# Feed-forward batches set to 18 turns against the recurrence's 32 phases, and the relaying of p and k moved from ScalarE to GpSimd

## The reference, cut to what matters

```python
def step(S, inp):                       # the recurrence, 512 tokens in order
    q_t, k_t, v_t = inp
    S = S * lam
    err = v_t - jnp.einsum('bhk,bhkv->bhv', k_t, S)
    S = S + beta * (k_t[..., :, None] * err[..., None, :])
    o_t = jnp.einsum('bhk,bhkv->bhv', q_t, S)
    return (S, o_t)
...
h = jax.nn.silu(_tlin(x, w1_w, w1_s)) * _tlin(x, w2_w, w2_s)      # the feed-forward
h = jax.nn.gelu(_tlin(h, h1_w, h1_s), approximate=False)
h = jax.nn.gelu(_tlin(h, h2_w, h2_s), approximate=False)
return _tlin(h, w3_w, w3_s)
...
x = x + _L0_attn_ref(xn, ...) + _L0_ffn_ref(xn, ...)
```

## Time and profile before

| | us |
|---|---|
| median of three runs | 954.16 |
| the profiled execution, whole | 952.11 |
| its span | 950.4 |
| DVE busy in the span | 780.1 |
| PE busy | 787.3 |
| POOL busy | 597.3 |
| ACT busy | 588.6 |

### The profile page before, as it was taken

One profiled execution on the slowest core, in us unless ns is written; L12 is line 12 of the kernel. 1 busy time (PEld: TensorE's weight loads), 2 busy tenths in 40 slices (PEclk: granted clock), 3 DMA queues, 4 the chain that ended last, 5 costly groups with the idle time before them and its releaser, 6 DMA issues. The chain is left out here.

```text
span 950.4 us, 12821 instructions
## 1 busy us (share of the span) xinstructions
PE 787.3 (83%) x2956; PEld 499.2 (53%) x2956; DVE 780.1 (82%) x1573; ACT 588.6 (62%) x1079; POOL 597.3 (63%) x542
## 2 busy tenths in 40 slices
PE   5388888266989898998988799874899999999996
PEld 3234343145655666665565666542455655555654
DVE  5588887199999999999999999912788888888885
ACT  3487877368878797877879787632444434443431
POOL 0078888264665555566655566412887878878873
PEclk9999999668999999999999999895999999999999
DMA  5145554900505023050504101023112312213201
GB/s 143 55 167 204 206 203 181 197 14 1 123 11 99 22 51 81 11 121 11 110 11 87 46 16 39 11 61 123 38 57 64 102 55 73 93 55 99 67 12 33
DMA packets 121652, 74.98 MB, mean 79 GB/s; under 512 B 73490, under 2 KB 99996, under 8 KB 121628
## 3 DMA queue, kind: packets, MB, share of 16 engines
q1 hardware_dynamic: 119420, 72.98, 27.3%
q10 hardware_dynamic: 2208, 1.74, 0.6%
HBM read 41.14 MB, written 33.55 MB: 79 GB/s over the span
## 5 line engine op out<-in xcount | busy, mean ns | idle before, releaser
L958 POOL TENSOR_TENSOR f_hl<-f_h,f_hh 128x512 fp32r<-128x512 f32 x64 | 81.9, 1296 | 113.3 <-ACT f_hh L1057 113.2
L1354 POOL TENSOR_TENSOR l_kv<-l_qkv 128x1024 f32<-128x1024 f32 x64 | 125.0, 1952 | 21.3 <-PE l_ps_s L1564 21.3
L966 POOL TENSOR_TENSOR f_g<-f_a,f_b 128x512 f32<-128x512 f32 x64 | 81.5, 1284 | 65.5 <-ACT f_b L1046 65.5
L1132 PE MATMUL f_ps<-f_gh,w_hi 128*128 128x512 f32 x256 | 105.0, 410 | 10.3 <-POOL f_gl L958 5.2
L1132 PE MATMUL f_ps<-f_xh,w_hi 128*128 128x512 f32 x128 | 58.2, 455 | 65.2 <-ACT f_a L1042 51.5
L1132 PE MATMUL f_ps<-f_hh,w_hi 128*128 128x512 f32 x256 | 107.8, 421 | 0.0
L933 DVE TENSOR_TENSOR r_pg<-r_rec,r_pt 128x512 f32<-128x512 f32 x128 | 88.5, 692 | 20.1 <-ACT r_kb L1002 14.4
L939 DVE TENSOR_REDUCE r_rec<-r_pg 128x64 f32<-128x576 f32 x128 | 97.4, 761 | 7.2
L1407 ACT ACTIVATE l_qkv<-l_ps_q 128x512 f32<-128x512 f32 x64 | 38.3, 598 | 103.3 <-PE l_ps_q L1551 103.3
L1485 DVE TENSOR_TENSOR l_qs<-l_ps_s,l_qd 128x1024 f32<-128x1024 f32 x64 | 78.2, 1221 | 24.1 <-PE l_ps_s L1564 22.8
L942 DVE TENSOR_TENSOR r_kw<-r_rec,r_kb 128x512 f32<-128x512 f32 x128 | 88.5, 691 | 4.5
(11 more groups left out here) (183 smaller groups left out, 1986.6 us busy)
## 6 DMA issues: line engine op xcount, KB each, us to landing
p_x<-in_L_attn_x_dram SPq DMA_DIRECT2D x16, 256.0 KB, 2.9
scratch_xnT<-p_xnT SPq DMA_DIRECT2D x16, 256.0 KB, 3.0
scratch_K<-p_kout SPq DMA_DIRECT2D x16, 256.0 KB, 2.9
scratch_fac<-p_fac SPq DMA_DIRECT2D x16, 256.0 KB, 2.0
scratch_R<-p_rr SPq DMA_DIRECT2D x16, 256.0 KB, 2.0
scratch_P<-p_pp SPq DMA_DIRECT2D x16, 256.0 KB, 2.1
f_x<-scratch_xnT SPq DMA_DIRECT2D x16, 256.0 KB, 2.9
r_p<-scratch_P SPq DMA_DIRECT2D x16, 256.0 KB, 4.7
```

The source lines that it names most:

```text
L958: pool.tensor_tensor(lower, full, upper.bitcast(F32), ALU.subtract).then_inc(done, 1)
L966: pool.tensor_tensor(g_f[:, j, :], a_f[:, j, :], b_f[:, j, :], ALU.mult).then_inc(gate_ok, 1)
L1132: nc.tensor.matmul(bank, c.w_hi[:, weights[k], :], upper[k], start=k == 0, stop=False)
L1354: pool.tensor_tensor(dst, k, v, ALU.mult).then_inc(kv_ok, 1)
```

## The change

Turns and phases are now tied by points. A turn has two points (its start, and before L1061 of before), 36 in all for 18 turns (16 batches and two turns of tail), and `serve` at point p serves phase p*32/36 - 1 (rounded down) if that is a new one. Four points after the first serve nothing. So turn 0 has no phase to serve, turn 5 and turn 14 have none at their start (points 10 and 28), and the last phases are served in the tail. `lay_r` now lays r two phases ahead of the saved one, as before.

The relaying of p and k is moved to POOL (`lay_p`, `lay_k`, tensor_copy), after the four `f_hl` of batches 1, 3, 5, 7, 10, 12 and 14 for segments 1 to 7. For segment 0 POOL lays p ahead of its first `f_xl`, and ACT lays k. DVE waits for two semaphores in place of one. The loops of ACT, POOL and SP over the batches are written out; those of PE and DVE are as before. SP's stores and loads are sorted to the new points.

```diff
@@ scalar
-                    save_w(s, 1)
-                    if not last:
-                        lay_r(s, 1)
+                    serve(n, 1)
...
+                def serve(n, half):
+
+                    ended = (2 * n + half) * NPH // POINTS - 1
+                    before = (2 * n + half - 1) * NPH // POINTS - 1
+                    if ended > before >= -1:
+                        save_w(ended)
+                        if ended + 2 < NPH:
+                            lay_r(ended + 2)
...
-                lay_pk(0)
-                lay(0, 0)
-                batch(Slot(0), first=True)
-                batch(Slot(1), second=True)
-                with act.Fori(0, 3) as it:
...
+                lay_r(0)
+                lay_first_k()
+                lay_r(1)
+                for n in range(SLOTS):
+                    batch(n)
+                serve(SLOTS, 0)
                 result(Slot(SLOTS - 2))
+                serve(SLOTS, 1)
                 for o in range(NB):
                     last_hidden(Slot(SLOTS - 1), o)
+                serve(SLOTS + 1, 0)
                 result(Slot(SLOTS - 1))
+                serve(SLOTS + 1, 1)
+                save_w(NPH - 1)
@@ gpsimd
+                def lay_p(seg):
+
+                    u = seg % 2
+                    pool.wait_ge(seg_in[u], 48 * G * (seg // 2 + 1))
+                    for g in range(G):
+                        ins = pool.tensor_copy(tok_p[u][:, g, :, :].rearrange("p (b i) k -> p b i k", i=BLK),
+                                               seg_p[u][:, g, :, :].rearrange("p k (i b) -> p b i k", i=BLK))
+                    ins.then_inc(p_laid, 1)
...
+                lay_p(0)
                 input_rest(Slot(0))
...
+                for n in range(SLOTS):
+                    batch(Slot(n), more=n < SLOTS - 1)
+                    for seg in range(1, NSEG):
+                        if ((seg - 1) * SEGPH + 2) * POINTS // NPH // 2 == n:
+                            lay_p(seg)
+                            lay_k(seg)
@@ vector
-                        dve.wait_ge(pk_laid, it * 2 + (u + 1))
+                        dve.wait_ge(p_laid, it * 2 + (u + 1))
+                        dve.wait_ge(k_laid, it * 2 + (u + 1))
```

More of the change, by code:

```diff
@@ L787, in recur_and_feed_forward @@
     RING = 6
+    POINTS = 2 * (SLOTS + 2)
     with ctx:
@@ L831, in recur_and_feed_forward @@
         w_out = [sem(f"r_w_out{u}") for u in range(2)]
-        pk_laid, r_laid, w_saved = sem("r_pk_laid"), sem("r_laid"), sem("r_w_saved")
+        p_laid, k_laid, r_laid, w_saved = sem("r_p_laid"), sem("r_k_laid"), sem("r_laid"), sem("r_w_saved")
         m1_ok, w_ok, m2_ok, gain_ok, s_ok = sem("r_m1_ok"), sem("r_w_ok"), sem("r_m2_ok"), sem("r_gain_ok"), sem("r_s_ok")
@@ L877, in _ @@
                 load(1, 1)
[L878 to L890, removed]
-                            if not last:
[L892 to L903, removed]
+                for n in range(SLOTS + 2):
+                    if n < SLOTS - 1:
+                        next_x(Slot(n))
+                    ends = [seg for seg in range(NSEG) if (seg + 1) * SEGPH * POINTS // NPH in (2 * n, 2 * n + 1)]
+                    late = [seg for seg in ends if (seg + 1) * SEGPH * POINTS // NPH == 2 * n + 1]
+                    if n >= 2 and late:
+                        store_y(Slot(n - 2))
+                    for seg in ends:
+                        if seg < NSEG - 2:
+                            load_after(seg, seg % 2)
+                        store(seg, seg % 2)
+                    if n >= 2 and not late:
+                        store_y(Slot(n - 2))
+                store(NSEG - 1, (NSEG - 1) % 2)
                 sp.wait_ge(y_out, 16 * SLOTS + 16)
@@ L974, in hidden_rest, with lay_k @@
                     rest(h_f[:, o, :], h_h[:, o, :], h_l[:, o, :], hl_ok)
+                def lay_p(seg):
[5 more added lines that the diff above has]
+                    ins.then_inc(p_laid, 1)
+                def lay_k(seg):
+                    u = seg % 2
+                    for g in range(G):
+                        ins = pool.tensor_copy(blk_k[u][:, g, :, :, :], seg_k[u][:, g, :, :].rearrange("p k (i b) -> p b k i", i=BLK))
+                    ins.then_inc(k_laid, 1)
                 def batch(s, more=True):
@@ L988, in batch, with lay_r @@
                         hidden_rest(s, o)
+                lay_p(0)
                 input_rest(Slot(0))
-                with pool.Fori(0, SLOTS - 1) as it:
-                    batch(Slot(0, it))
-                batch(Slot(SLOTS - 1), more=False)
+                for n in range(SLOTS):
[4 more added lines that the diff above has]
+                            lay_k(seg)
             @block.scalar
             def _(act):
[L997 to L1008, removed]
+                def lay_r(phase):
+                    seg, at, q = phase // SEGPH, phase % SEGPH, phase % 2
+                    u = seg % 2
+                    if at == 0:
+                        act.wait_ge(seg_in[u], 48 * G * (seg // 2 + 1))
+                    if phase >= 2:
+                        act.wait_ge(w_ok, PH * (phase - 1))
                     act.activation(pg[q][:, :, :, :, DH].rearrange("p a vg i -> p vg a i"),
@@ L1011, in lay, with save_w, lay_first_k @@
                                    ACT.Copy).then_inc(r_laid, 1)
-                def lay_r(s, half):
-                    ahead = 2 * s.off + 1 + half
-                    u, at = (ahead // SEGPH) % 2, ahead % SEGPH
+                def save_w(phase):
+                    seg, at, q = phase // SEGPH, phase % SEGPH, phase % 2
+                    u = seg % 2
                     if at == 0:
[L1018 to L1030, removed]
+                        act.wait_ge(w_out[u], 16 * G * (seg // 2 + 1))
+                    act.wait_ge(s_ok, PH * (phase + 1) + 1)
                     act.activation(seg_w[u][:, :, :, at * TPH:at * TPH + TPH].rearrange("p v g t -> p (v g) t"),
                                    w_of[q], ACT.Copy).then_inc(w_saved, 1)
+                def lay_first_k():
+                    for g in range(G):
+                        ins = act.activation(blk_k[0][:, g, :, :, :], seg_k[0][:, g, :, :].rearrange("p k (i b) -> p b k i", i=BLK), ACT.Copy)
+                    ins.then_inc(k_laid, 1)
+                def serve(n, half):
[5 more added lines that the diff above has]
+                            lay_r(ended + 2)
                 def input_upper(s):
@@ L1066, in result, with batch @@
                     act.activation(y_t[:, :], y_at[:, :], ACT.Identity, scale=c.s3[:, :], bias=c.ob[:, :]).then_inc(y_ok, 1)
[L1068 to L1071, removed]
+                def batch(n):
+                    s = Slot(n)
+                    first, second, last = n == 0, n == 1, n == SLOTS - 1
+                    serve(n, 0)
                     silu(s, 0)
```

9 lines of the change are left out of this document (removed).

## The result

The changed kernel takes 941.6 us (median of 6 runs, 938.5 to 942.7) against 954.2 for the kernel before beside it (6 runs, 952.6 to 957.5): ratio 0.987, 95% interval 0.985 to 0.989, 12.6 us faster. The forecast was 950.0.

A forecast was written before the change was run, and what follows sets the result against it. DVE's recurrence was taken as the bound, with the feed-forward tail to win: 12.8 us less 1.1 lateness and 7.5 low clock is 4.2, so 947.9 profiled, stated as 950 against the 954.16 median; range 941 to 965.

The forecast's parts named there:

- The bound: DVE's recurrence bounds the stage while it runs: 434.6 us, 13.56 per phase; 17.0 us of feed-forward tail follow it.
- The end: After the recurrence, save and W stores take 5.4 us until the next stage's first load.
- The start: With POOL laying p beside ACT's r and k, DVE starts the recurrence at about 186.3, 1.3 us earlier.
- The turn without copies: An ACT turn without relaying needs 24.0 us, read from turn 12, with nothing left over at the new pace.
- The price of an output at low clock: PE's output takes 5.39 us instead of 3.69 when the granted clock falls, costing 1.7 us.
- the slower rival, copies too slow: POOL's copies become the bound: gain gone at 1.48 us a copy, 29 us slower at 2.7; chance 0.20.
- the turn with relaying on POOL: Four copies of 1.3 us make the gates 2.6 to 2.8 us late and six turns 25.4 us.
- the 1.1 us of lateness: At point 29, in turn 14's second half, service comes at 539.2 where DVE wants it at 538.1.
- the 7.5 us of low clock: PE's pauses ahead of z1 of j=3 lower the clock over outputs: 5.7 us plus 1.8 us.
- The formula for the turn: ACT's chain in a turn with copies: 27.08 - 4.07 (relaying) - 0.22 (wait for DVE) + 2.6 (gates late) = 25.4 us.
- the recurrence alone: Rival: clock holds or copies are near 1.07 us, 11.7 to 12.8 us won, time 942; chance 0.20.
- the alternation of turns: Sign: ACT's turns alternate between 24.0 and 25.4 us, or 25.7 where the output runs at low clock.

The follow-up runs named there:

- experiment 1: The changed kernel with the old pacing of 32 points instead of 36, relaying of p and k still on POOL: 953.86 us, ratio 0.998 to the kernel before.
- experiment 2: The changed kernel with 36 points, but p and k of segments 1 to 7 relaid by ACT again: 966.38 us, ratio 1.011 to the kernel before.
- experiment 4: The changed kernel with three unused copies more in each relaying on POOL, seven in all, 7.0 us: 958.15 us, ratio 1.003 to the kernel before.
- experiment 3: The changed kernel with a fifth, unused copy in each relaying on POOL, 5.1 us: 944.73 us, ratio 0.989 to the kernel before.
- experiment 5: The changed kernel with one unused ACT instruction of 0.57 us at the start of each turn: 946.65 us, ratio 0.993 to the kernel before.

## Why the prediction was wrong

**What held.** The bound: the recurrence is never faster than its 13.6 us per phase, and the gain can be no more than the tail less the last store (12.8 by the sum, 12.4 at equal landing). The end: 5.0 us, 5.4 forecast. The start: 1.3 us. The turn without copies: 24.0 us, read from one turn. The pace at which the points come due: 435.3/18 = 24.2 us, so these turns just fit. The price of an output at low clock: 1.7 us. Both parts of the change are needed (experiments 1 and 2), and the slower rival, copies too slow, is real with its waits at the very places (experiment 4), only from a price on that POOL doesn't have.

**The step that failed** is the turn with relaying on POOL: "I take 1.3, in the middle of the near ones", and with it 25.4 us for six turns, where 24.0 were measured; the 1.1 us of lateness and the 7.5 us of low clock were worked out from it, and both came to nothing. A copy takes 1.07 to 1.09 us by its groups and 1.01 from one to the next, which is the prediction's own lower bound, worked out from what is fixed in the two-input rows. That bound was the better supported one: the upper one supposed that nothing of a copy's 402 ns is fixed, against what those rows showed, and a fixed part hidden behind the operation before, the reason given for 1.3, speaks for less and not for more. That 1.07 was met to 0.01 us is luck in part, since the fixed part was borrowed from another operation. By the Trainium skill (GPSIMD Engine Reference, section 7: some 2.9 cycles per element for reads with a step over 8 bytes) a copy was estimated at 1.34 us. The runs don't agree for this form: 30 copies of 512 rearranged elements stand at 1.07 to 1.09, and the measurement decides.

**What hung on it.** The gates come 1.9 us late instead of 2.6 to 2.8. The formula for the turn then has another 0.75 us too much, as experiments 3 and 4 show, and the traces show most of it. It added the delay in full, but the second save comes 1.5 us late and not 1.9: ACT's own waits for the gates take up 0.36. And turn 11 of before did wait for DVE at its end, which the prediction denied. These rows of before stand ahead of the save at 513.44:

```profile
512.54 0.77 ACT L1057 ACTIVATE f_hh<-f_ps,t 128x512 fp32r<-128x512 f32 x1
513.04 0.36 DVE L952 SCALAR_TENSOR_TENSOR r_rec<-r_rec,lam,r_gain 128x128 f32<-128x128 f32 x1
```

The save starts 0.90 us behind the last `f_hh`, where 0.57 is usual, and right behind the end of DVE's block at 513.40; that is 0.33. So the turn with copies is 24.0, as the others. From that two terms fall. The lateness at point 29, 1.1 us: six turns shorter by 1.4 would have left ample room, but the wait for DVE at turn 9 and the low output behind it take most of it back; the serving there is at 538.72 where DVE wants it at 539.4, 0.7 us ahead. And the clock, 7.5 us, the largest term: it was priced with PE's pause of 1.9 us behind turns made longer by the copies. No such turn was left; the pauses are 1.42 us and the clock stays in all eleven. The argument (a pause of 1.9 us brings the fall in part of the turns, at 1.7 us each) stood the test of experiment 5, with 4 of 12 instead of 4 of 6.

**How much was the price.** The duration of a copy does not explain the whole miss. Experiment 3 has the 5.1 us of relaying that the prediction took, and it measured 944.7 where the prediction said 950; so of the 8.4 us between 950.0 and 941.6 the price accounts for 3.1. The other 5.3 are in what was built on it: in experiment 3 six turns are 0.5 us shorter than the 25.4 (2.8 us), and the low clock took some 5 us in three turns where 7.5 were set (2.5 us). This split is an estimate from that one trace.

**The chances.** The case that came true, the recurrence alone at 942, was written out with its condition, "copies near 1.07", and 0.20. Since three terms hung on one unknown price whose near bounds were 1.07 and 1.61, the forecast was a middle between cases that don't occur together: at 1.07 all three vanish, above 1.3 all grow, and at 1.3 itself the time would have been near 945. The time lies just inside the range. Of the signs named, the W store last, the start and the 24.0 came; the alternation of turns, DVE's 5 to 10 us of waits and the 1.3 us copies did not.

## What to carry to other kernels

When work is moved into another engine's gap, the number that matters is the slack of the turn, and whether the turn stays within it is a matter of yes or no: here 4.05 us of copies cost nothing, 5.1 cost 3 us and 7.0 cost 16.5, with 0.1 us of room in the turn at the first. Work out from which duration on the next engine sets the turn, and give the chances by the side of that point on which the unknown price falls, with all terms that depend on it together. And when two loops share queues, pace the shorter so that its turn at the longer one's speed is just what it can do: the copies on POOL alone (experiment 1) gained nothing, the pacing alone (experiment 2) cost 12 us, and together they gained 12.6.

## What the runs showed of the hardware

- A copy with rearranged elements, 128x512 in 32 bits, takes 1.07 us on POOL (`L967`) and took 1.15 on ACT (1.10 to 1.13 in the mean of its 32); in order it takes 0.68 there. For this form GpSimd is no slower than ACT.
- PE's pause ahead of the output and the granted clock in it: 1.42 us, 11 of 11 outputs at the upper level in the changed kernel; 1.65 us in experiment 3, 3 of 4 low; 1.9 us, 4 of 6 low before and 4 of 12 in experiment 5. Over all twelve traces: pauses of 1.41 to 1.44 us, none of 86 low; 1.62 to 1.67, 6 of 10; 1.88 to 1.91, 8 of 18; 2.19 and longer, 30 of 32. The length of the pause alone doesn't decide. Half a microsecond more of waiting on another engine can thus cost 1.7 more on PE, though not every time.
- DVE's instructions of the recurrence kept their durations (358 to 361 ns for the last of a block) with POOL's copies beside them.
